# First batch of a four-stage conditional kernel: another queue for two weights, x added on TensorE for all row tiles, a small tile for the empty matmuls

## The reference, cut to what matters

```python
h = relu(x @ w1 + b1)                          # w1: 256 x 64, of the language
adapted = h @ w2 + b2                          # w2: 64 x 256
x = x + layernorm(x + adapted) * gamma + beta  # of the language
x = x + (x @ W[subject].T + b[subject])        # W: 256 x 256, of the subject
x = x + mixture(x, type)                       # five nets 256 -> 1024 -> 256, gated
x = x + attention_pool(x, type)
```

## Time and profile before

| | us |
|---|---|
| median of 3 runs | 497.57 |
| lowest, highest | 497.13, 498.37 |
| the profiled execution, its own time | 497.3 |
| its span in the trace | 495.5 |
| PE busy in the span | 488.9 (99%) |
| DVE, ACT, POOL busy | 368.7, 260.6, 239.4 |

### The profile page before, as it was taken

How to read it: one execution, slowest core, us unless ns; L and a number is a source line. 1 busy time by engine, 2 the same in 40 slices (tenths; PEclk the granted TensorE clock), 3 DMA queues, 4 the chain that set the end, 5 groups by cost and what they waited for, 6 DMA issues and landing times.

```text
span 495.5 us, 6989 instructions
## 1 busy us (share of the span) xinstructions
PE 488.9 (99%) x2296; PEld 404.8 (82%) x2296; DVE 368.7 (74%) x750; ACT 260.6 (53%) x506; POOL 239.4 (48%) x201
## 2 busy tenths in 40 slices
PE   8999999999999999999999999999999999999996
PEld 5788888888888888888888888888888888888985
DVE  5688237997687799989578689899678779644477
ACT  4655555544457574535346666444455757445243
POOL 1575446456254446454644437444635444746023
PEclk9999999999999999999999999999999999999999
DMA  5965354322255442422237454422222342340002
GB/s 159 186 188 148 101 144 148 105 87 85 87 124 147 117 113 86 128 86 86 85 89 186 108 177 112 127 87 85 86 85 86 103 110 85 100 135 22 1 1 85
DMA packets 77657, 52.97 MB, mean 107 GB/s; under 512 B 40758, under 2 KB 67382, under 8 KB 77622
## 3 DMA queue, kind: packets, MB, share of 16 engines
q1 hardware_dynamic: 75734, 50.44, 36.2%
q10 hardware_dynamic: 1888, 2.10, 1.4%
HBM read 48.33 MB, written 2.10 MB: 102 GB/s over the span
## 4 chain that ended last, share of the span: by engine, by line
PE 96%; DVE 2%; issue 0%; ACT 0%; POOL 0%; DVEq 0%
PE ps_hid L830 15%; PE ps_hid L835 15%; PE ps_hid L831 15%; PE ps_net L892 14%; PE ps_net L887 14%; PE ps_net L888 14%; PE ps_net L859 2%; PE ps_side L538 1%; PE ps_side L542 1%; PE ps_side L537 1%; PE ps_side L548 1%; PE ps_side L551 1%; PE ps_hid L686 1%; PE ps_net L665 1%; PE ps_hid L637 0%; PE ps_hid L777 0%
## 5 line engine op out<-in xcount | busy, mean ns | idle before, releaser
L1928 POOL TENSOR_TENSOR wi_lo<-raw_wi,wi_hi 128x512 fp32r<-128x512 f32 x77 | 103.3, 1342 | 208.6 <-ACT wo_hi L1077 111.4
L1098 ACT ACTIVATE hid_hi<-ps_hid 128x512 fp32r<-128x512 f32 x160 | 95.7, 599 | 188.9 <-PE ps_hid L835 187.0
L1831 DVE SCALAR_TENSOR_TENSOR hid_lo<-ps_hid,hid_hi 128x512 fp32r<-128x512 f32 x160 | 109.6, 688 | 91.1 <-ACT hid_hi L1098 89.4
L830 PE MATMUL ps_hid<-x2T_hi,wi_lo 128*128 128x512 f32 (+1 forms) x332 | 125.3, 379 | 0.0
L831 PE MATMUL ps_hid<-x2T_hi,wi_hi 128*128 128x512 f32 (+1 forms) x332 | 125.1, 379 | 0.0
L887 PE MATMUL ps_net<-hid_hi,wo_hi 128*128 128x512 f32 x304 | 118.7, 391 | 0.0
L888 PE MATMUL ps_net<-hid_hi,wo_lo 128*128 128x512 f32 x304 | 118.5, 390 | 0.0
L1929 POOL TENSOR_TENSOR wo_lo<-raw_wo,wo_hi 128x512 fp32r<-128x512 f32 x77 | 105.6, 1371 | 0.0
L835 PE MATMUL ps_hid<-x2T_lo,wi_hi 128*128 128x512 f32 (+1 forms) x332 | 98.9, 379 | 0.0
L892 PE MATMUL ps_net<-hid_lo,wo_hi 128*128 128x512 f32 x304 | 93.9, 390 | 0.0
L831 PEld LDWEIGHTS ps_hid<-x2T_hi,wi_hi 128*128 128x128 f32 x332 | 62.4, 188 | 12.0
(11 more groups left out here) (328 smaller groups left out, 509.5 us busy)
## 6 DMA issues: line engine op xcount, KB each, us to landing
raw_wi<-in_L_cond_share_wi_dram SPq DMA_DIRECT2D x23, 512.0 KB, 3.8
raw_wo<-in_L_cond_share_wo_dram SPq DMA_DIRECT2D x23, 512.0 KB, 4.8
raw_wi<-in_L_cond_expert_wi_dram SPq DMA_DIRECT2D x16, 512.0 KB, 3.8
raw_wo<-in_L_cond_expert_wo_dram SPq DMA_DIRECT2D x16, 512.0 KB, 4.8
next_x2T<-in_x_dram SPq DMA_DIRECT2D x24, 64.0 KB, 4.3
x_rows<-in_x_dram SPq DMA_DIRECT2D x3, 512.0 KB, 4.1
x_rows<-netT SPq DMA_DIRECT2D x48, 32.0 KB, 2.0
out_dram<-out_rows SPq DMA_DIRECT2D x5, 256.0 KB, 5.7
```

The source lines that it names most:

```text
L830: mm(dst, wi_lo[:, w, k, c], x2T_hi[:, k, rows], start=(k == 0), stop=False)
L1098: fn(hid_hi[:, ring(b, q)], ps_hid[:, ring(b, q)], ACT.Relu).then_inc(hid_hi_ready, 1)
L1831: v.scalar_tensor_tensor(out=hid_lo[:, ring(b, q)], in0=ps_hid[:, ring(b, q)], scalar=0.0, in1=f32(hid_hi[:, ring(b, q)]), op0=ALU.max, op ...
L1928: g.tensor_tensor(wi_lo[:, w], raw_wi[:, half % 2, :, c], f32(wi_hi[:, w]), ALU.subtract)
```

## The change

The language's w2 is sent by ACT, which now reads the language's identifier in place of the subject's. The subject's weights are sent by SP, right after it has read the subject's identifier. In the prologue PE adds x for all four tiles with the identity, DVE's two additions are gone, and DVE normalises the odd tiles from PSUM. PE's order becomes: x of tile 0, hidden 0, x of tile 1, adapted 0 and 1, hidden 1, x of tiles 2 and 3, adapted 2 and 3. The hidden layer gets banks of its own. DVE writes variance plus epsilon ahead of the negated mean, and POOL waits for the latter ahead of the shift. The empty matmuls read a 128 x 128 bfloat16 tile of zeros that is cleared first, repeated four times as the moving operand.

```diff
-        zeros = edge_diag[:, 0:S // 2].bitcast(BF16)
+        zeros = sb("zeros", [P, P], BF16)
...
+        def hidden_bank(h):
+            return (ps_hid[0:A, 2], ps_net[0:A, 2])[h][:, 0:HS]
...
-                    sp.dma_start(w2[:], L0_W2[la].rearrange("o a d -> (o a) d")).then_inc(w2_in, 16)
+                    if not (isinstance(i, int) and i == 0):
+                        sp.dma_start(w2[:], L0_W2[la].rearrange("o a d -> (o a) d")).then_inc(w2_in, 16)
...
-                if not (isinstance(i, int) and i == 0):
+                if isinstance(i, int) and i == 0:
+                    sp.dma_start(subj_w[:], L1_weight[su].rearrange("o (k p) d -> p (o k) d", p=P)).then_inc(subj_in, 16)
+                else:
                     load_blocks(subj_blocks, L1_weight[su], subj_in)
...
-                for h in range(2):
-                    adapter_hidden(h)
-                    for r in (2 * h, 2 * h + 1):
-                        adapted_rows(r)
+                add_x(0)
+                adapter_hidden(0)
+                add_x(1)
+                adapted_rows(0)
+                adapted_rows(1)
+                adapter_hidden(1)
+                add_x(2)
+                add_x(3)
+                adapted_rows(2)
+                adapted_rows(3)
                 pe.wait_ge(subj_in, 16)
...
+            def add_x(r):
+                mm(adapted_bank(r), ident[:], x_rows[:, r], start=True, stop=False)
...
-                    mm(bank, zeros[:, 0:P], zeros[:], start=True, stop=True)
+                    mm(bank.rearrange("p (o c) -> p o c", c=P), zeros[:], zeros[:].rearrange("p (o c) -> p o c", o=1).to_broadcast([P, R, P]), start=True, stop=True)
...
-            subj = act.value_load(subj_id.rearrange("(o b) -> o b", o=1)[0:1, 0:1], min_val=0, max_val=L1_weight.shape[0] - 1)
+            lang = act.value_load(lang_id.rearrange("(o b) -> o b", o=1)[0:1, 0:1], min_val=0, max_val=L0_W1.shape[0] - 1)
+            act.dma_start(w2[:], L0_W2[bass.ds(lang, 1)].rearrange("o a d -> (o a) d")).then_inc(w2_in, 16)
...
-            act.dma_start(subj_w[:], L1_weight[bass.ds(subj, 1)].rearrange("o (k p) d -> p (o k) d", p=P)).then_inc(subj_in, 16)
...
-                    rows = adapted_bank(r)
-                    if r % 2:
-                        done(v.tensor_tensor(norm[:, r], adapted_bank(r), x_rows[:, r], ALU.add))
-                        here(f"sum{r}")
-                        rows = norm[:, r]
-                    done(v.bn_stats(stats[:, r], rows))
+                    done(v.bn_stats(stats[:, r], adapted_bank(r)))
...
-                    v.tensor_scalar(neg_mean[:, rows], aggr[:, rows, 0], -1.0, None, ALU.mult)
                     done(v.tensor_scalar(var_eps[:, rows], aggr[:, rows, 1], LN_EPS, None, ALU.add))
+                    done(v.tensor_scalar(neg_mean[:, rows], aggr[:, rows, 0], -1.0, None, ALU.mult))
...
-            v.memset(edge_diag[:], 0.0).then_inc(zeros_ready, 1)
+            v.memset(zeros[:], 0.0).then_inc(zeros_ready, 1)
             v.memset(ones[:], 1.0).then_inc(zeros_ready, 1)
             v.memset(hT[A:A + 1], 1.0).then_inc(zeros_ready, 1)
+            v.memset(edge_diag[:], 0.0)
```

More of the change, by code:

```diff
@@ L286, in cond_resid_program @@
         p_act = Steps(sem("p_act"), "xT0 xT1 hid0 xb0 hid1 xb1 norm0 subj_wT norm1")
-        p_dve = Steps(sem("p_dve"), "stats0 sum1 stats1 aggr0 var_eps0 stats2 norm0 sum3 stats3 aggr1 var_eps1 x1T00 x1T01 norm1 x1T10 x1T11")
+        p_dve = Steps(sem("p_dve"), "stats0 stats1 aggr0 var_eps0 neg_mean0 stats2 norm0 stats3 aggr1 var_eps1 neg_mean1 x1T00 x1T01 norm1 x1T10 x1T11")
         p_pool = Steps(sem("p_pool"), "rstd0 shift0 rstd1 shift1")
@@ L636, in adapter_hidden @@
                 for k in range(KD):
-                    last = mm(ps_hid[0:A, h, 0:HS], w1[:, k], x1T[:, k, rows_half(h)], start=(k == 0), stop=(k == KD - 1))
+                    last = mm(hidden_bank(h), w1[:, k], x1T[:, k, rows_half(h)], start=(k == 0), stop=(k == KD - 1))
                 last.then_inc(p_pe.sem, 1)
+            def add_x(r):
+                mm(adapted_bank(r), ident[:], x_rows[:, r], start=True, stop=False)
             def adapted_rows(r):
[L642 to L651, removed]
+                pe.wait_ge(p_act.sem, p_act.at(0, f"hid{r // 2}"))
+                if r == 0:
+                    pe.wait_ge(zeros_ready, 3)
+                    pe.wait_ge(w2_in, 16)
+                    pe.wait_ge(b2_in, 16)
+                mm(adapted_bank(r), hT[:, tile_cols(r)], w2b[:], start=False, stop=True).then_inc(p_pe.sem, 1)
             def normalised_rows(h):
@@ L1139, in adapter_hidden @@
                 act.wait_ge(p_pe.sem, p_pe.at(0, f"hid{h}"))
-                fn(hT[0:A, rows_half(h)], ps_hid[0:A, h, 0:HS], ACT.Relu, bias=b1[:]).then_inc(p_act.sem, 1)
+                fn(hT[0:A, rows_half(h)], hidden_bank(h), ACT.Relu, bias=b1[:]).then_inc(p_act.sem, 1)
             def x_beta(h):
@@ L1765, in normalise @@
                     dve.wait_ge(p_pool.sem, p_pool.at(0, f"rstd{h}"))
-                    done(v.tensor_scalar(norm[:, r], norm[:, r], aggr[:, r, 0:1], rstd[:, r:r + 1], ALU.subtract, ALU.mult))
+                    done(v.tensor_scalar(norm[:, r], adapted_bank(r), aggr[:, r, 0:1], rstd[:, r:r + 1], ALU.subtract, ALU.mult))
                 def add_norm(h):
@@ L1959, in _ @@
                 pool.wait_ge(p_pool.sem, p_pool.at(0, f"rstd{h}"))
+                pool.wait_ge(p_dve.sem, p_dve.at(0, f"neg_mean{h}"))
                 g.tensor_tensor(neg_shift[:, r], neg_mean[:, r], rstd[:, r], ALU.mult).then_inc(p_pool.sem, 1)
```

## The result

The changed kernel has a median of 498.89 us over 22 runs (498.03 to 499.38), the kernel before 497.49 over as many. The ratio is 1.0021, with a 95% interval of 1.0015 to 1.0026: 0.2% slower, 1.0 us by the ratio (1.1 between the means, 498.77 and 497.67) and 1.4 by the medians. The forecast was 498.2 and "within 0.3%". The profiled execution took 499.04 us, its span 496.9 (before: 497.3 and 495.5).

A forecast was written before the change was run, and what follows sets the result against it. PE, busy 99% of the span, was taken as the bound, the end following M. Leg B put M at 15.6, 0.9 later; less 0.15 to 0.2 absorbed, +0.7 us gave a median of 498.2, range 497.2 to 499.3.

The forecast's parts named there:

- M: Moment PE begins the prologue's last transposes, those of half 1: 14.72 us before, forecast 15.6, 0.9 later.
- leg B: PE's own queue from the landing of the subject's weights to M: 3.3 us, giving M = 15.6.
- I take 12.3: Landing of the subject's weights on SP's queue, in us, between bounds of 11.3 and 13.4.
- PE starts 0.25 earlier: Program start: clearing the smaller zeros tile takes 0.13 us in place of 0.38, so PE's empty matmuls begin 0.25 earlier.
- I take 5.6: Start of the hidden layer of half 0, in us, as now; x of tile 0 uses up the earlier start.
- leg A: DVE's statistics of half 1, then variance, power, shift and normalising up to M: 14.6, 0.1 earlier.
- add_x(3) ahead of adapted 2: PE's prologue queue: tile 3's x pair comes first, 0.43 us, so DVE gets tile 2 at 11.2.
- the whole saving is given back: DVE's prologue queue: the removed sums gain nothing; statistics 3 start at 11.95 against 11.94 now.
- The 0.2 wait of rows 3 takes up 0.15: PE's 0.2 us wait for DVE's x2T_lo behind the prologue absorbs 0.15 to 0.2 of M's delay.
- the kernel's end moves one for one with M: Behind the prologue PE runs from its own queue, so any shift of M shifts the end equally.
- rival 2: Slower by over 0.3%: subject's weights move only after ACT's megabyte, landing 13.8, M 17.1, time 499.8; chance 0.08.
- Rival 1: Subject's weights share the engines and land before 11.4; 0.1 to 0.25 us gained, 497.4; chance 0.18.

The follow-up runs named there:

- experiment 3: Changed kernel with the two loads put back (w2 on SP, subject's weights on ACT); ratio 1.0015 to the kernel before.
- experiment 12: Kernel of 10 with the two loads exchanged (w2 on ACT, subject's weights on SP); ratio 1.0007 to the kernel before, median 498.21 us.
- 10: Changed kernel without the loads' exchange, x of tile 0 behind the hidden layer, DVE's counts in slots 9 to 12, gate's loads later; ratio 0.9984, median 496.94 us.
- experiment 1: Kernel before with only the two loads exchanged (w2 on ACT, subject's weights on SP); ratio 1.0031, median 499.33 us.
- experiment 4: Changed kernel with ACT's megabyte of net weights issued behind its first two additions of beta; ratio 1.0019 to the kernel before.
- experiment 9: Kernel before with small zeros tile, DVE's counts in slots 9 to 12, variance before negated mean, gate's loads later; ratio 0.9986, median 497.03 us.
- experiment 5: Kernel before with only the small tile of zeros; ratio 0.9994.
- experiment 11: Changed kernel with the two loads put back and the gate's loads later; ratio 0.999 to the kernel before.
- experiment 6: Changed kernel with the two loads put back and x of tile 0 added behind the hidden layer; ratio 1.0008 to the kernel before.
- experiment 2: Kernel before with the two loads exchanged and eight empty matmuls ahead of PE's wait for the subject's weights; ratio 1.0015.
- experiment 7: Kernel before with the small tile of zeros and DVE's counts moved from slots 5 and 6 to slots 9 to 12; ratio 0.9991.

## Why the prediction came out as it did

The step that gave the direction was right: a wait for subj_w ahead of its transposes becomes the bound of M, and the end is later by less than 0.3%. The form of leg B was confirmed three times: M is the landing plus 3.3 (13.15 and 16.42, 12.8 and 16.07, 12.5 and 15.75). Inside the 3.3, terms were off by up to 0.3 and cancelled: the subject's transposes took 0.94 and not 1.25, the way from the transposes of half 0 to DVE's sum 0.72 and not 0.5, from there to the subject products 0.63 and not 0.49.

That all the rest nearly cancels was wrong for the change as it stands. Without the exchange it still lost 0.7 us between the means (experiment 3), of the 1.1 with it, and the intervals of the two ratios overlap: in this kernel the runs do not tell what the exchange adds. Its price shows where the other losses are gone, in experiment 12 against 10.

So there is luck in the number. M came 0.8 later than forecast. Nearly 0.4 us came around the span, which the forecast had as unchanged. Against this, 0.25 was absorbed at 39.6 us in the profiled pair, and the other runs of the kernel before are often longer than its profiled one (495.2 to 497.6 us of span beside experiment 1, where the profile has 495.5). Between the means about 0.7 us are left within the span, the forecast's figure with other terms.

The mis-sized term is the landing. "I take 12.3" measured 13.15. Three parts of it were off. SP's issue was at 7.93 and not 8.5, because SP's second identifier took 1.5 us in place of 2.0. ACT's megabyte was issued at 7.33 and not 6.9, since it follows the hidden layer. And the transfer took 5.2 us, not 3.8. The stretches of the changed kernel show the engines full from 10 to 12 us:

```profile
9.00:10.00 1.00, 1.00 (x5) 0.46 (x5) 0.92 (x6) 0.12 (x1) 0.00 (x0) 1.00 0.82 305
10.00:11.00 1.00, 1.00 (x5) 0.90 (x6) 0.00 (x0) 0.99 (x3) 0.85 (x2) 1.00 1.04 384
11.00:12.00 1.00, 0.90 (x5) 0.44 (x3) 0.49 (x2) 0.66 (x2) 0.06 (x1) 1.00 1.09 387
12.00:13.00 1.00, 0.00 (x0) 0.00 (x0) 0.97 (x4) 0.00 (x0) 0.00 (x0) 1.00 0.84 203
```

At 385 GB/s the 1.31 MB (512, 512 and 256 KB of 1024 bytes) of the two streams fill 3.4 us, whatever the order. These are the same bytes as before. There they were issued from 6.93 on and the last landed at 13.1; now they are issued from 7.33 on, and raw_wo landed at 7.74 + 5.6 = 13.3, subj_w at 13.15. I had counted subj_b's 4.2 us from an issue 0.6 earlier, as if they were a duration of its own, and had then taken the lower end of 12.3 to 12.7. The DMA queues from 11 to 12 us (packets, MB, share of 16 engines; q10 is ACT's, q1 SP's):

```profile
q10 hardware_dynamic: 197, 0.20, 56.7%
q1 hardware_dynamic: 181, 0.19, 52.2%
```

SP's queue moved nothing from 8 to 10.5 us and 0.01 MB from there to 11, three microseconds behind its issue at 7.93; then it had half of the engines, until its 256 KB were through by 12.5. The Trainium skill ("DMA: Bandwidth & Descriptors", Queues, rings and completion order) says that each engine alternates between the queues that have work. The equal shares from 11 to 12 us agree with it, and so I was wrong to read subj_b's 4.2 us as strict order. But I was wrong as well to say that by this rule the landing would be near 11.3: the small transfer got its share only from about 11 us on, and then half the rate. Why its packets came so late is not shown; with ACT's loads issued at its side in experiment 4 it took 4.1 us, and on ACT's queue ahead of the megabyte 2.8.

"PE starts 0.25 earlier", "the transposes 0.2 earlier": 0.34 and 0.3, near enough. "I take 5.6" for the hidden layer measured 6.13, and that is the step that failed in the sum of leg A. I let the clock's rise move with PE's start. It came at 5.9 us where it had been 4.9, though PE began earlier. It varies from one execution to the next: eight transposes at 421 to 447 ns here and in experiment 9, a median of 273 in experiment 5, with the same start of PE. From the pair of matmuls ahead of the hidden layer to that layer it was 0.52 us in experiment 11, where the clock rose early, and 0.84 and 0.99 in the changed kernel and experiment 3, where it rose late; with the pair behind it the hidden layer began at 5.42 though the clock rose only at about 5.35 (experiment 6). The sentence "through before the hidden layer" was true of the transposes, and not of the pair behind them.

"add_x(3) ahead of adapted 2" and "the whole saving is given back": right. Statistics 2, normalise 0 and statistics 3 followed each other without a pause, 11.51, 11.85, 12.30, all about 0.3 later than I said, behind a hidden layer that was 0.5 late. Normalising from PSUM took 0.53 where I took 0.40 to 0.45, 0.1 more.

"The 0.2 wait of rows 3 takes up 0.15": that one stayed, at 0.2. What was absorbed is the wait for hid_lo at 39.6, 0.25 us of PE's time, which I had read and passed over. Rows 3 said that PE is not bound by its own queue alone behind the prologue; the sentence "the kernel's end moves one for one with M" is false, and most of all toward the fast side. Experiment 5 loses there what it wins in the prologue.

The prediction's own signs: it had a wait of 0.7 us for the weights and called itself wrong over 1.7. PE's weight load waited 1.70 and PE itself 1.29, which is at that edge. There was no new wait behind 24 us, as it said.

The measured landing, 13.15, is at the edge from which rival 2 was to decide, and the time stayed under its 0.3% because M moved by 1.7 and the span by only 1.4.

Rival 1 did not come: no landing before 11.4 was seen with the exchange. Rival 2's mechanism, the transfer behind a megabyte that is no earlier, came about in part (13.3 for the megabyte), with M 0.7 short of its price. A case I had not listed is the fallen clock in the wait. In the exchange alone it happened in half of the runs and cost 2.5 us. In the changed kernel no run was above 499.38 or had a mean granted clock under 0.997, so that it did not come there. There PE's adapter matmuls end at 11.9, since x of tiles 2 and 3 stands among them, and its pause has 1.29 us; in experiment 1 they end at 11.4 and the pause has 1.69. The first lines of the two timelines behind the pause, of the changed kernel:

```profile
13.19 0.33 PE L573 MATMUL ps_net<-ident,subj_w 128*128 128x128 f32 x1 [1.29 <-DMA subj_w<-in_L_cond_weight_dram]
```

and of experiment 1, with the first transpose at half clock:

```profile
13.07 0.48 PE L569 MATMUL ps_net<-ident,subj_w 128*128 128x128 f32 x1 [1.69 <-DMA subj_w<-in_L_cond_weight_dram]
```

That the shorter pause spared the changed kernel was not tried by itself and stays open.

## What to carry to other kernels

When two queues share the engines, price a moved transfer by the bytes that all queues have in flight until its end, not by its own latency, and issue first what is waited for first. Where PE is busy for 99% of the span, the few waits that are left are seams between stages: a gain ahead of a seam can be given back there, so read the waits behind the edit before the sum is made, and move what holds them (here the gate's megabyte, by one line) with the edit. Work on PE ahead of a stage that others wait for may run at half clock early in a program; put it behind that stage's first product.

## What the runs showed of the hardware

The granted clock fell from full to half in a pause of PE of 1.69 us, and the six runs with a mean granted clock of 0.995 or 0.996 are 2.5 us longer than the other six (experiment 1). With eight empty matmuls in the wait it stayed full (experiment 2), and in pauses of 1.29 and 1.24 us too (the changed kernel, experiment 12). At the start of the program the same code saw the rise at about 4.7 us in one kernel and 6.6 in another, whose programs differ only in the place of the gate's loads (experiments 11 and 3). One read of an identifier from memory by SP (pointer and value) took 1.5 us in the changed kernel, 2.0 in the kernel before and 3.4 in experiment 7, and shifted everything queued behind it. A 256 KB load on SP's queue moved its first bytes some 3 us after its issue while ACT's megabyte was under way, and then shared the engines evenly with it. A DVE operation on 4 columns takes 0.23 us while POOL is idle, and 1.2 when it starts about 0.1 us into a split of 1.3 us. And the time around the span was 1.8 us in some of these kernels and 2.2 in others, for a reason that no run shows.
